# Layer norms of a two-layer transformer: statistics taken chunk by chunk, and three of eight chunks normalised on one engine

## The reference, cut to what matters

```python
def _layernorm(x, axis=-1, eps=1e-05):
    m = jnp.mean(x, axis=axis, keepdims=True)
    v = jnp.var(x, axis=axis, keepdims=True)
    return (x - m) / jnp.sqrt(v + eps)
...
h = _layernorm(x) * (1 + ca) + sa
x = x + ga * _L0_attn_ref(h, ...)   # normalises h again; 16 heads, relative positions, softmax
h = _layernorm(x) * (1 + cb) + sb
x = x + gb * _L0_ffn_ref(h, ...)    # 8 experts, 2 chosen a token, all 8 computed
h = _layernorm(x) * (1 + ca) + sa   # second layer, its own ca, sa, cb, sb
x = x + ga * _L1_attn_ref(h, ...)   # linear attention
h = _layernorm(x) * (1 + cb) + sb
x = x + gb * _L1_ffn_ref(h, ...)    # gated layer, inputs and weights rounded to FP4 in blocks of 16
```

## Time and profile before

| | |
|---|---|
| median of 3 runs | 1256.58 us (1253.76 to 1261.54) |
| profiled execution | 1258.67 us, its span 1256.9 us |
| PE busy | 905.8 us (72%) |
| DVE busy | 808.6 us (64%) |
| ACT busy | 464.3 us (37%) |
| POOL busy | 328.4 us (26%) |
| chain that ended last | PE 49%, DVE 18%, ACT 8%, DMA 6%, POOL 5% |
| mean granted clock of PE | 0.883 |

### The profile page before, as it was taken

One profiled execution on the slowest core, in us unless ns is written; L12 is line 12 of the kernel. 1 busy time (PEld: TensorE's weight loads), 2 busy tenths in 40 slices (PEclk: granted clock), 3 DMA queues, 4 the chain that ended last, 5 costly groups with the idle time before them and its releaser, 6 DMA issues.

```text
span 1256.9 us, 22649 instructions
## 1 busy us (share of the span) xinstructions
PE 905.8 (72%) x8587; PEld 668.4 (53%) x8587; DVE 808.6 (64%) x1632; ACT 464.3 (37%) x745; POOL 328.4 (26%) x361
## 2 busy tenths in 40 slices
PE   0149587999899999953379999999936880257674
PEld 0123476888788788743235655655523770145453
DVE  1735353554455455412768888888886868989885
ACT  0365032333333333322845555555544123111211
POOL 6552000233233323355800000000036035211211
PEclk9769798999999999986679999999977995587876
DMA  9005511332233233211300000000000000000000
GB/s 120 0 19 140 178 36 26 72 77 60 66 71 67 60 71 77 52 46 23 100 1 2 1 0 0 0 0 0 0 15 0 1 1 17 1 0 17 17 17 17
DMA packets 68829, 46.10 MB, mean 37 GB/s; under 512 B 34489, under 2 KB 60065, under 8 KB 68033
## 3 DMA queue, kind: packets, MB, share of 16 engines
q1 hardware_dynamic: 51600, 24.05, 9.6%
q0 software_dynamic: 8448, 19.81, 6.3%
q10 hardware_dynamic: 8704, 1.19, 0.6%
HBM read 30.05 MB, written 12.06 MB: 34 GB/s over the span
## 4 chain that ended last, share of the span: by engine, by line
PE 49%; DVE 18%; issue 9%; ACT 8%; DMA 6%; POOL 5%; ACTq 3%; SPq 1%; POOLq 0%; DVEq 0%
PE PS L801 7%; PE PS L876 5%; PE PS L878 5%; PE PS L877 5%; PE PS L821 4%; PE PS L781 4%; PE PS L782 4%; PE PS L805 3%; ACTq L598 3%; PE PS L753 3%; ACT HN L566 2%; DMA YC<-queries_content 2%; DVE STAT L1037 2%; DVE HB L1235 2%; PE PS L1012 1%
## 5 line engine op out<-in xcount | busy, mean ns | idle before, releaser
L1118 DVE TENSOR_REDUCE MX<-PS 128x2 f32<-128x512 f32 x256 | 170.8, 688 | 197.5 <-PE PS L782 196.0
L618 ACT ACTIVATE REG<-PS 128x1024 f32<-128x1024 f32 x128 | 131.3, 1026 | 254.1 <-PE PS L805 251.3
L801 PE MATMUL PS<-XP,TB 96*128 96x64 f16 x2048 | 159.7, 246 | 1.6 <-DMA XC<-NEG 1.6
L781 PE MATMUL PS<-TM,YP 128*128 128x256 f16 x512 | 129.6, 285 | 40.9 <-DMA YC<-queries_content 22.9
L801 PEld LDWEIGHTS PS<-XP,TB 96*128 96x128 f16 x2048 | 130.9, 120 | 29.3 <-issue 21.5
L782 PE MATMUL PS<-KM,YC 128*128 128x256 f16 x512 | 125.8, 278 | 0.0
L876 PE MATMUL PS<-XH,W 128*128 (+1 forms) x256 | 99.1, 387 | 24.6 <-DVE HB L1235 24.6
L661 ACT ACTIVATE SG<-PS 128x512 f32<-128x512 f32 x128 | 76.3, 597 | 106.0 <-PE PS L878 105.7
L1235 DVE SCALAR_TENSOR_TENSOR HB<-PS,SG 128x512 f32<-128x512 f32 x128 | 87.1, 686 | 35.3 <-ACT SG L661 33.1
L805 PE MATMUL PS<-XC,KC 97*128 97x128 f16 x1024 | 107.3, 228 | 0.0
L781 PEld LDWEIGHTS PS<-TM,YP 128*128 128x128 f16 x512 | 73.3, 143 | 49.9 <-DMA YC<-queries_content 25.3
(11 more groups left out here) (229 smaller groups left out, 1760.6 us busy)
## 6 DMA issues: line engine op xcount, KB each, us to landing
REG<-inverse_sums POOLq DMA_DIRECT2D x64, 128.0 KB, 3.1
YC<-queries_content ACTq DMA_DIRECT2D x224, 4.0 KB
KC<-keys_strips SPq DMA_DIRECT2D x16, 192.0 KB
keys_strips<-REG POOLq DMA_DIRECT2D x12, 224.0 KB, 8.0
R<-in_L_attn_x SPq DMA_DIRECT2D x8, 256.0 KB, 13.3
R<-REG POOLq DMA_DIRECT2D x64, 32.0 KB, 2.5
out<-R SPq DMA_DIRECT2D x64, 32.0 KB, 1.6
queries_position<-REG POOLq DMA_DIRECT2D x2, 960.0 KB, 8.7
```

The costliest lines, as they stand in the source:

```text
L618: A(P[jt][:, 1024 * up:1024 * up + 1024].rearrange("p (k x) -> p k x", k=2), ST[u % 2], ACT.Exp).then_inc(exp_done, 1)
L781: mm(o, yp[:, a], TM[p][:, 31 - a:31 - a + T], start=True, stop=False)
L801: mm(o_pos[:, a], TB[p][0:96, y0:y0 + 128], xp[0:96, 8 * bank + a], start=(a == 0), stop=False, skip_group_check=True)
L1118: nc.vector.tensor_reduce(MX[h % 2][:, 2 * kk:2 * kk + 2], banks[4 + kk % 2].rearrange("p (a j) -> p a j", a=2), AX_X, ALU.max)\
```

## The change

- The statistics are split into chunk_statistics (four bn_stats) and moments (the seven small operations a half).
- Before norms 3 and 5 chunk_statistics of a chunk stands in DVE's queue behind the gate product of the next chunk. The first half's moments stand behind the fifth gate product.
- Norm 4's bn_stats move into finish, behind the addition onto R2, with tile numbers from the loop's register.
- Chunks 3, 6 and 7 of each norm are normalised by DVE alone: four tensor_scalar instructions (plus the negated mean, times the inverse root), and, outside norm 2, the multiplication and the addition of the shift. ACT and POOL do chunks 0, 1, 2, 4, 5.
- In modulated DVE takes, in each half, its own chunks first and ACT's after them. In norm 2 its chunks stand behind both moments and before the weight copies.

```diff
+BY_ACT, BY_DVE = (0, 1, 2, 4, 5), (3, 6, 7)
...
+        def wait_normalised(eng, order, c):
+
+            if c in BY_ACT:
+                eng.wait_ge(norm_act, 5 * (order - (order > 0)) + BY_ACT.index(c) + 1)
+            else:
+                eng.wait_ge(norm_dve, 3 * order + BY_DVE.index(c) + 1)
+
...
-            def shifted(order, dst, shift, ready):
-
-                for c in range(8):
-                    gp.wait_ge(scale_done, 8 * order + c + 1)
+            def shifted(order, dst, shift):
+
+                for i, c in enumerate(BY_ACT):
+                    gp.wait_ge(scale_done, 5 * order + i + 1)
                     t = dst[:, 4 * c:4 * c + 4, :]
-                    gp.tensor_tensor(t, t, shift.unsqueeze(1).to_broadcast([128, 4, D]), ALU.add).then_inc(ready, 1)
+                    gp.tensor_tensor(t, t, shift.unsqueeze(1).to_broadcast([128, 4, D]), ALU.add).then_inc(norm_act, 1)
...
-            gp.wait_ge(h_ready, 8)
+            gp.wait_ge(h_ready, 5)
+            gp.wait_ge(norm_dve, 6)
...
-            def centre(k, src, dst, done, before=0):
-
-                for n in range(NT):
-                    if n % (NT // 2) == 0:
-                        act.wait_ge(rstd_ready, 2 * k - 1 + n // (NT // 2))
-                    last = A(dst[:, n, :], src[:, n, :], ACT.Identity, bias=LN[:, 3, n:n + 1], scale=LN[:, 2, n:n + 1])
-                    if n % 4 == 3:
-                        last.then_inc(done, 1)
+            def centre(k, src, dst, done):
+
+                for c in BY_ACT:
+                    if c % 4 == 0:
+                        act.wait_ge(rstd_ready, 2 * k - 1 + c // 4)
+                    for n in range(4 * c, 4 * c + 4):
+                        last = A(dst[:, n, :], src[:, n, :], ACT.Identity, bias=LN[:, 3, n:n + 1], scale=LN[:, 2, n:n + 1])
+                    last.then_inc(done, 1)
...
+                    if src is HN:
+                        if c in BY_ACT:
+                            pe.wait_ge(h_ready, BY_ACT.index(c) + 1)
+                        else:
+                            pe.wait_ge(norm_dve, 3 + BY_DVE.index(c) + 1)
+                    elif src is XQ:
+                        pe.wait_ge(xq_ready, c + 1)
+                    else:
+                        wait_normalised(pe, k + 1, c)
...
-            def statistics(src, half):
-
-                tiles = slice(NT // 2 * half, NT // 2 * (half + 1))
-                for n in range(tiles.start, tiles.stop):
+            def chunk_statistics(src, c):
+
+                for n in range(4 * c, 4 * c + 4):
                     last = nc.vector.bn_stats(STAT[:, n, :], src[:, n, :])
                 step(last)
+
+            def moments(half):
+
+                tiles = slice(NT // 2 * half, NT // 2 * (half + 1))
                 me, mo = STAT[:, tiles, 1], STAT[:, tiles, 4]
...
-            def scaled(order, dst, scale):
-
-                for c in range(8):
-                    ve.wait_ge(centred, 8 * order + c + 1)
-                    t = dst[:, 4 * c:4 * c + 4, :]
-                    TT(t, t, scale.unsqueeze(1).to_broadcast([128, 4, D]), ALU.mult).then_inc(scale_done, 1)
+            def modulated(k, order, src, dst, scale, shift):
+
+                for half in range(2):
+                    for c in BY_DVE:
+                        if c // 4 == half:
+                            ve.wait_ge(rstd_ready, 2 * k - 1 + half)
+                            for n in range(4 * c, 4 * c + 4):
+                                last = TS(dst[:, n, :], src[:, n, :], LN[:, 0, n:n + 1], LN[:, 2, n:n + 1], ALU.add, ALU.mult)
+                            step(last)
+                            t = dst[:, 4 * c:4 * c + 4, :]
+                            step(TT(t, t, scale.unsqueeze(1).to_broadcast([128, 4, D]), ALU.mult))
+                            TT(t, t, shift.unsqueeze(1).to_broadcast([128, 4, D]), ALU.add).then_inc(norm_dve, 1)
+                    for i, c in enumerate(BY_ACT):
+                        if c // 4 == half:
+                            ve.wait_ge(centred, 5 * (order - (order > 0)) + i + 1)
+                            t = dst[:, 4 * c:4 * c + 4, :]
+                            TT(t, t, scale.unsqueeze(1).to_broadcast([128, 4, D]), ALU.mult).then_inc(scale_done, 1)
...
+            modulated(1, 0, R2, HN, MOD[0][:, 1, :], MOD[0][:, 0, :])
+            for c in range(8):
+                wait_normalised(ve, 0, c)
+                chunk_statistics(HN, c)
+                if c % 4 == 3:
+                    moments(c // 4)
+            for c in BY_DVE:
+                ve.wait_ge(rstd_ready, 3 + c // 4)
+                for n in range(4 * c, 4 * c + 4):
+                    last = TS(HN[:, n, :], HN[:, n, :], LN[:, 0, n:n + 1], LN[:, 2, n:n + 1], ALU.add, ALU.mult)
+                last.then_inc(norm_dve, 1)
...
             for c in range(8):
                 ve.wait_ge(o_mm, c + 1)
                 gate_projection(c, banks[2 + c % 2], MOD[0][:, 2, :], TMP[c % 2], o_mul, o_add)
...
-            for half in range(2):
-                ve.wait_ge(o_add, 4 * half + 4)
-                statistics(R2, half)
-            scaled(1, HN1, MOD[0][:, 4, :])
+                if c:
+                    ve.wait_ge(o_add, c)
+                    chunk_statistics(R2, c - 1)
+                if c == 4:
+                    moments(0)
+            ve.wait_ge(o_add, 8)
+            chunk_statistics(R2, 7)
+            moments(1)
+            modulated(3, 2, R2, HN1, MOD[0][:, 4, :], MOD[0][:, 3, :])
...
                 ve.wait_ge(cmbt, 3 * tc + 2)
                 x4 = R2[:, bass.ds(4 * tc, 4), :]
                 TT(x4, x4, ACC2[:, :, :], ALU.add).then_inc(cmbt, 1)
+                ve.wait_ge(cmbt, 3 * tc + 3)
+                for j in range(4):
+                    n = bass.ds(4 * tc + j, 1)
+                    last = nc.vector.bn_stats(STAT[:, n, :], R2[:, n, :])
+                last.then_inc(stat_done, 1)
...
+            ve.wait_ge(stat_done, 8)
             for half in range(2):
-                statistics(R2, half)
-            scaled(2, HN2, MOD[1][:, 1, :])
+                moments(half)
+            modulated(4, 3, R2, HN2, MOD[1][:, 1, :], MOD[1][:, 0, :])
...
             for c in range(8):
                 ve.wait_ge(l_o, c + 1)
                 gate_projection(c, banks[4 + c % 2], MOD[1][:, 2, :], CT[c % 2][:, :], l_mul, l_od)
+                if c:
+                    ve.wait_ge(l_od, c)
+                    chunk_statistics(R2, c - 1)
+                if c == 4:
+                    moments(0)
+            ve.wait_ge(l_od, 8)
+            chunk_statistics(R2, 7)
+            moments(1)
...
-            for half in range(2):
-                ve.wait_ge(l_od, 4 * half + 4)
-                statistics(R2, half)
...
-            scaled(3, HN3, MOD[1][:, 4, :])
+            modulated(5, 4, R2, HN3, MOD[1][:, 4, :], MOD[1][:, 3, :])
             w = HN3[:, :, :].rearrange("p n (k s) -> p (n k) s", s=16)
             BLOCKS = NT * D // 16 // 4
             for c in range(4):
                 k = slice(BLOCKS * c, BLOCKS * (c + 1))
-                ve.wait_ge(pre_ready, 8 + 2 * c + 2)
+                wait_normalised(ve, 4, 2 * c)
+                wait_normalised(ve, 4, 2 * c + 1)
                 t = [QS[j][:, :].rearrange("p (k s) -> p k s", s=16)[:, k] for j in range(2)]
                 rounded, scale = quantise(w[:, k], t[0], t[1], [AM[j][:, k] for j in range(3)])
                 step(rounded)
-                TT(XQ[:, :, :].rearrange("p n (k s) -> p (n k) s", s=16)[:, k], t[0], scale, ALU.mult).then_inc(h_ready, 2)
```

More of the change, by code:

```diff
@@ L228, in adaln_program @@
             "f_w", "f_tr", "f_ev", "f_gu", "f_sg", "f_h", "f_ht", "f_hv", "f_y", "f_out"))
+        xq_ready, stat_done = sem("xq_ready"), sem("stat_done")
         stored = sem("stored")
@@ L504, in _ @@
             inverse_root(3)
-            shifted(1, HN1, MOD[0][:, 3, :], h_ready)
+            shifted(1, HN1, MOD[0][:, 3, :])
             for e in range(E):
@@ L519, in _ @@
             inverse_root(4)
-            shifted(2, HN2, MOD[1][:, 0, :], h_ready)
+            shifted(2, HN2, MOD[1][:, 0, :])
             gp.wait_ge(ld_l1, 128)
@@ L526, in _ @@
             inverse_root(5)
-            shifted(3, HN3, MOD[1][:, 3, :], pre_ready)
+            shifted(3, HN3, MOD[1][:, 3, :])
             gp.wait_ge(t_evac, 25)
@@ L1084, in _ @@
             ve.sem_inc(mod_ready, 1)
-            scaled(0, HN, MOD[0][:, 1, :])
-            for half in range(2):
-                ve.wait_ge(pre_ready, 4 * half + 4)
-                statistics(HN, half)
+            modulated(1, 0, R2, HN, MOD[0][:, 1, :], MOD[0][:, 0, :])
+            for c in range(8):
+                wait_normalised(ve, 0, c)
+                chunk_statistics(HN, c)
+                if c % 4 == 3:
+                    moments(c // 4)
+            for c in BY_DVE:
[3 more added lines that the diff above has]
+                last.then_inc(norm_dve, 1)
             ve.wait_ge(pe_prep, 3)
@@ L1372, in _ @@
```

(2 more changed lines are left out.)

6 lines of the change are left out of this document (3 added, 3 removed).

## The result

The changed kernel took 1280.28 us (median of 4 runs, 1279.43 to 1282.02) beside 1258.99 us for the kernel before (median of 4, 1253.76 to 1261.54). The ratio is 1.0181, with a 95% interval of 1.0147 to 1.0216. So the kernel became slower by 21 us by the medians and 23 us by the ratio, where 10 were forecast and 1277 was the end of the range.

What follows compares the result with a forecast made beforehand. PE was taken to bound the expert loop, and a relay of DVE, POOL, ACT and PE the norms. Terms 7.0 - 1.5 - 0.6 + 2.0 + 2.2 + 0.6 = +9.7 us gave 1266.3 us, own range 1258 to 1274, wider range 1255 to 1277.

Steps and rivals of the forecast that it cites:

- Statistics at 1.0 us a round: Expert loop: four bn_stats ahead of the HB product lengthen each of seven joined rounds; +7.0 us, bounds +5.6 and +10.5.
- PE has no slack to win it back: Expert loop: PE is the bound, busy 32.21 of 35.00 us, so DVE work before the HB product lengthens the round.
- the dense work around the stop speaks against a fall, the longer stop for it: Expert loop: weighing whether PE's stop, growing from 1.92 to about 2.9 us, makes the clock fall; chance 0.20.
- the rival: Expert loop: the clock falls behind PE's longer stop, 2.5 us a fall, +8.7 in half the rounds: 1275 us; chance 0.20.
- Norm 4: Behind the experts: statistics come early, but DVE's own chunks set the pace; gain 1.5 us, bounds 3.5 and a loss of 1.
- rival 4: Norms 4 and 5: four DVE scalings take 0.8 us, 1.8 us less in all: 1264.5 us, 1262.8 by page's price; chance 0.12.
- Norm 3: Norm 3: late additions close POOL's hole, and ACT's first weight chunk comes at 613.6 instead of 614.3; -0.6 us, bounds ±1.5.
- The last addition was forecast 3.2 us late: Norm 3: statistics between gate products make POOL's last addition end at 599.2 instead of 596.0.
- rival 3: Norms 2, 3, 4: ACT's 4.7 us come off the path in full, plus norm 4 and 5 gains; -12.5, 1244 us; chance 0.08.
- Norm 5: FN's quantisation waits for a later load, +2.0 us; the norm takes 48.8 instead of 46.7, +2.2, bounds -1.2 and +5.
- Norms 1 and 2: Weight copies behind DVE's chunks delay PE; first projection near 89.1 instead of 88.46; +0.6 us, bounds -1 and +3.

Runs made afterwards that it cites:

- e4: Changed kernel with eight unused matmuls more on PE in each joined round, where PE stops at a round's end: 1273.12 us, ratio 1.0143.
- e1: Changed kernel without the four bn_stats of each loop round; norm 4 takes its 32 statistics behind the loop: 1267.1 us, ratio 1.009.
- e3: Changed kernel with a round's four bn_stats moved, one tile behind each of experts 3 to 6 of the next round: 1266.19 us, ratio 1.007.
- e5: Kernel of e1 with all eight chunks of a norm scaled by ACT, as before the change: 1258.12 us, ratio 1.0004.
- e6: Kernel of e1 with the statistics of norms 3 and 5 behind all gate products; DVE's share of three chunks stays: 1264.51 us, ratio 1.005.
- e9: Kernel of e6 with 24 one-element ACT copies, read by nothing, between norms 1 and 2: 1260.32 us, ratio 1.0036.
- e7: Kernel before, with gating multiplication and R2 addition moved behind the products of experts 2 and 3 in seven joined rounds: 1251.03 us, ratio 0.9928.
- e8: Kernel of e7 with norm 4's statistics too, one tile behind each of experts 4 to 7 of the next round: 1251.9 us, ratio 0.9964.
- e2: Kernel before, with only the four bn_stats behind each loop round's R2 addition and norm 4's moments from them: 1269.44 us, ratio 1.0102.

## Why the prediction was wrong, by its own steps

**The loop.** Statistics at 1.0 us a round: right (0.95). That PE has no slack to win it back: right, e4 loses exactly that in each round. Wrong was the step from there: "the dense work around the stop speaks against a fall, the longer stop for it", with a chance of 0.20. The clock fell in 5 of 7 stops of 2.87 us, in three traces out of three, and in none of the stops of 1.92 to 1.94 us in the kernel before, e1, e3, e5, e6 and e9. The step took its evidence from two rows at the wrong lengths: PE's stop of 1.92 us, and that of the earlier trace rows, which lasted 6.77 us (PE came back at 193.29). The trace of the kernel before had one much nearer to 2.9 us, a wait of 2.47 us between two heads. PE's timeline, and the windows behind the restart:

```profile
317.61 0.33 PE L781 MATMUL PS<-TM,YP 128*128 128x256 f16 x1 [2.47 <-DMA YC<-queries_content]
```

```profile
317.61:318.61 1.00, 1.00 (x7) 0.85 (x8) 0.00 (x0) 0.00 (x0) 0.00 (x0) 0.59 0.33 103
318.61:319.61 1.00, 1.00 (x12) 1.00 (x11) 0.69 (x1) 0.00 (x0) 0.00 (x0) 0.50 0.37 68
```

The clock fell to half behind it, and so it did at that boundary in all thirteen traces (stops of 2.2 to 2.9 us). Length alone does not settle it: in the attention of the kernel before, a stop of 1.58 us (to 164.03) was followed by half clock too. The size given to the rival, 2.5 us a fall in half of the rounds, was 8.7 us; 5 at 1.65 us make 8.25. That the two totals agree is luck, since the falls were more and each was smaller. Had it been the forecast, it would have said 1275, still 5 us short of 1280 for want of the attention.

**The first attention.** No step of the prediction looked at it, because nothing of the change is in it. It grew by 5.7 us in the profile, of which about 4 us pass at the boundary near 342 us: the Exp instructions start 2.4 us early (against before) at 318 us, 1.5 us late at 346 us. e9 takes this part away, with the limits said there. The rest, about 2 us, is a fall behind a 1.84 us wait at 394 us. No other trace has it at that boundary, but three have one like it elsewhere (e4 at 517, e7 at 462, e8 at 436 us). I take it for chance, as I do the load's -2.8 us (the first statistic comes at 22.1 to 27.8 us in the thirteen traces); neither is shown.

**Norm 4** (-1.5 forecast, -1.85 measured) went as walked through. Timeline of the changed kernel, which answers to the earlier trace rows:

```profile
943.51 0.87 DVE L1296 BATCH_NORM_STATS2 STAT<-R 128x6 f32<-128x128 f32 x4
...
945.65 2.98 POOL L434 TENSOR_TENSOR LN<-LN 128x16 f32<-128x16 f32 x1 [3.41 <-DVE LN L1068]
...
948.97 7.80 ACT L577 ACTIVATE HN<-R,LN 128x128 f32<-128x128 f32 x20 [11.25 <-POOL LN L436]
948.97 1.11 DVE L1077 TENSOR_SCALAR HN<-R,LN 128x128 f32<-128x128 f32 x4 [2.41 <-POOL LN L436]
...
954.47 3.02 DVE L1077 TENSOR_SCALAR HN<-R,LN 128x128 f32<-128x128 f32 x4
...
958.87 1.11 DVE L1077 TENSOR_SCALAR HN<-R,LN 128x128 f32<-128x128 f32 x4
...
961.35 1.28 DVE L1086 TENSOR_TENSOR HN<-HN,MOD 128x512 f32<-128x512 f32 x2
962.11 2.87 POOL L443 TENSOR_TENSOR HN<-HN,MOD 128x512 f32<-128x512 f32 x2 [5.21 <-DVE HN L1086]
...
968.70 3.63 PE L939 MATMUL PS<-R,L1W 128*128 128x512 f32 x4 [0.69 <-ACT R L679]
```

ACT is done with its scalings at 956.8; DVE takes chunks 6 and 7 from 954.47 to 961.35, before the multiplications of chunks 4 and 5, and POOL stands idle for 5.21 us for them. Four scalings take 1.11 us, the 1.1 that the PSUM row gave, and 3.02 us when POOL's additions are under way. The Trainium skill (VectorE: DVE Perf Modes, section on the TRN2 errata) prices four of them at an estimated 0.51 us; the measurement decides, and rival 4 is out. In the 3.02 us two of the four scalings took 1.30 us each, where the median of all is 0.34, and the last two ran once POOL had ended at 956.90; an addition takes 1.25 us undisturbed. The Trainium skill's rule of an exclusive lock between DVE and GpSimd (SBUF — State Buffer, SBUF: two separate sides) agrees with that: each of the two is held for the rest of one addition. All of the gain is the statistics'; the share itself loses 0.8 us here (e2 against the changed kernel).

**Norm 3** (-0.6, bounds ±1.5; measured -1.7 with the stretch behind it). The last addition was forecast 3.2 us late:

```profile
598.57 1.27 POOL L459 TENSOR_TENSOR R<-REG,R 128x512 f32<-128x512 f32 x1 [1.62 <-DVE REG L1211]
...
601.58 1.26 POOL L459 TENSOR_TENSOR R<-REG,R 128x512 f32<-128x512 f32 x1 [0.24 <-DVE REG L1211]
602.80 2.92 POOL L434 TENSOR_TENSOR LN<-LN 128x16 f32<-128x16 f32 x1
...
606.06 7.80 ACT L577 ACTIVATE HN<-R,LN 128x128 f32<-128x128 f32 x20 [9.55 <-POOL LN L436]
...
616.37 1.97 PE L876 MATMUL PS<-CON,WGN 128*128 128x128 f32 x8 [16.61 <-DMA RN<-in_L_ffn_router_w]
...
617.53 0.60 ACT L650 ACTIVATE W<-PS 128x512 f16<-128x512 f32 x1 [3.66 <-PE PS L876]
```

Counted from ACT's first copy of the attention's result (585.68, before 581.35) it is 2.5 us late (17.2 instead of 14.65 us), POOL's hole of 2.65 us is closed, and ACT starts at the same distance as before. The weights reach PE 2.8 us later, and ACT, free at 613.86, waits 3.66 us for them. So the mechanism held, and e6 shows what it hid: with the additions on time the share is worth 3.7 us. What rival 3 said of ACT's 4.7 us comes near the truth in this norm, without the statistics between the products, and in no other.

**Norm 5** (+2.0 for FN, +2.2 for itself; measured +1.7 and +3.1):

```profile
1058.10 0.43 SPq L408 DMA_DIRECT2D FN<-in_L_ffn_w_down  x1
...
1060.56 0.95 DVE L1395 TENSOR_REDUCE AM<-FN 128x48 f32<-128x768 f32 x1 [3.41 <-DMA FN<-in_L_ffn_w_down]
...
1075.58 1.10 DVE L1077 TENSOR_SCALAR HN<-R,LN 128x128 f32<-128x128 f32 x4
...
1080.92 3.01 DVE L1077 TENSOR_SCALAR HN<-R,LN 128x128 f32<-128x128 f32 x4
...
1088.98 1.21 DVE L1395 TENSOR_REDUCE AM<-HN 128x64 f32<-128x1024 f32 x1
```

DVE is busy from 1075.58 to 1088.98 with what was to take 13.8 us (13.4). The excess lies in the four quarters, 36.4 us instead of 35.0: the first starts while POOL's last two additions run. A slip of the sum is in it too: four undisturbed quarters by its own rows are 4 x 8.82 = 35.3 us, so the term should have read +2.4.

**Norms 1 and 2** (+0.6, measured +1.3). PE's L745 came 53.18 us behind the first statistic instead of 43.82, 9.4 us later (8.4 forecast), and almost all of it was hidden, as said. The path was the one forecast, DVE's chunks and the weight copies behind them; the term was 0.7 us too small. DVE's part in norm 1 starts 23.85 us behind the first statistic instead of 22.98, 0.9 us that the forecast did not count, and 0.8 of them are norm 1's two groups of 16 statistics at 3.6 instead of 3.2 us. (The working also carries the growth of 11.30 to 13.6 us on as 2.7 instead of 2.3; measured, this stretch grew from 11.22 to 13.42.)

**The sum.** Loop +7.9 more than forecast, first attention +5.7, norm 5 and FN +0.6, norms 1 and 2 +0.7, norms 3 and 4 -1.5, and -2.1 in stages that no part of the change touches: 9.7 + 11.3 = 21.0 us.

## What to carry to other kernels

Put new work of an engine behind the instruction that another one waits for, not ahead of it: the same four instructions cost 0.19 us a round in one place and 2.1 us in the other, with the falls of the clock. When an edit lengthens a regular stop of PE, look through the whole trace for stops near the new length and price the clock's fall with those, not with the stop of the old length. Give a share of work to a second engine only where it can do it ahead of what others wait for: here that paid in one norm of five. And read stages that were not edited too: here a shorter stream on one engine went with a packet of instructions moved into a gap, and a longer stop there.

## What the runs showed of the hardware

- In this loop PE's clock fell behind 15 of 21 stops of 2.86 to 2.87 us (the changed kernel twice, e2) and in none of 42 stops of 1.92 to 1.94 us (the kernel before, e1, e3, e5, e6, e9). Filled to 1.14 us of idleness: none of 7. A fall cost 1.65 us a time. Outside the loop the same length is no safe measure: it also fell behind a stop of 1.58 us in the first attention (kernel before) and one of 1.84 us (changed kernel).
- Statistics of 128x128 tiles: sixteen in a run take 3.19 us, four 0.87 us, and four whose addresses come from a register 1.00 us.
- An 8 KB packet of the instruction queue in the gap between two heads went with a stop of 2.8 to 3.4 instead of 1.1 us, in six traces of six; 24 more instructions on ACT moved the packet and took the stop away. The boundary before has a stop of 2.2 to 2.9 us with no such packet in all thirteen traces.
- A DVE scaling of a 128x128 tile with two values per partition, SBUF to SBUF, takes 0.34 us, and four in a row 1.11. In the changed kernel the same four took 3.01 to 3.02 us beside POOL's additions, in norms 1, 3, 4 and 5 alike, and 3.99 us in norm 4 of e1.
